# Key tokens by the DMA queue's transposes in place of TensorE's, in a 16-sequence mLSTM and ternary feed-forward block

## The reference, cut to what matters

```
q, k, v = x @ Wq.T, x @ Wk.T, x @ Wv.T           # 256, 256, 512 features
i, f    = soft_cap(x @ Wig.T + big), soft_cap(x @ Wfg.T + bfg)
per token: m' = max(log_sigmoid(f) + m, i);  F = exp(log_sigmoid(f) + m - m');  I = exp(i - m')
           C  = F C + I k v^T;  n = F n + I k
           h  = (q/sqrt(32) . C) / (max(|q/sqrt(32) . n|, exp(-m')) + eps)
x = x + (sigmoid(x @ Wog.T) * head_norm(h) * gamma) @ Wout.T
x = x + gelu(layer_norm(x) @ t(w1).T + b1) @ t(w2).T + b2      # t: absmean ternary
```

## Time and profile before

| what | value |
|---|---|
| time, median of 3 runs | 1792.62 us (1792.32 to 1792.75) |
| profiled execution, its own time | 1793.07 us |
| its span, first to last instruction | 1791.3 us |
| PE busy | 1742.3 us (97%), 12184 matmuls |
| DVE busy | 1412.3 us (79%) |
| ACT busy | 1069.6 us (60%) |
| POOL busy | 604.4 us (34%) |
| mean granted TensorE clock | 0.988 |

### The profile page before, as it was taken

One profiled execution on the slowest core, in us unless ns is written; L12 is line 12 of the kernel. 1 busy time (PEld: TensorE's weight loads), 2 busy tenths in 40 slices (PEclk: granted clock), 3 DMA queues, 4 the chain that ended last, 5 costly groups with the idle time before them and its releaser, 6 DMA issues.

```text
span 1791.3 us, 31686 instructions
## 1 busy us (share of the span) xinstructions
PE 1742.3 (97%) x12184; PEld 868.2 (48%) x12184; DVE 1412.3 (79%) x2526; ACT 1069.6 (60%) x1801; POOL 604.4 (34%) x481
## 2 busy tenths in 40 slices
PE   5879999999999999999999999999999999999999
PEld 3454444444444444444444454444444444444555
DVE  6787878788787878878887887877878787886872
ACT  6877638375573737557373764737466483756743
POOL 1241332524334251432525143252424325242340
PEclk9879999999999999999999999999999999999999
DMA  8433335261432625243262424426243352515120
GB/s 289 167 101 93 85 88 141 54 150 51 122 85 58 163 57 142 62 120 89 54 163 59 128 69 113 106 54 159 54 119 82 97 127 54 133 47 125 32 54 24
DMA packets 255846, 177.76 MB, mean 99 GB/s; under 512 B 200128, under 2 KB 221632, under 8 KB 250576
## 3 DMA queue, kind: packets, MB, share of 16 engines
q1 hardware_dynamic: 254112, 172.59, 37.5%
q10 hardware_dynamic: 1584, 3.15, 0.5%
HBM read 96.47 MB, written 20.23 MB: 65 GB/s over the span
## 4 chain that ended last, share of the span: by engine, by line
PE 74%; ACT 13%; DVE 7%; issue 2%; POOL 1%; DMA 0%; POOLq 0%; DVEq 0%; ACTq 0%
PE pf L2047 23%; PE pf L2031 15%; PE pa L1884 13%; PE pa L1860 9%; PE psh L1884 7%; ACT dec L960 6%; ACT sig L919 2%; DVE gT L1574 2%; PE psh L1987 2%; DVE dec L1460 2%; ACT gT L996 1%; PE pa L1851 1%; ACT L993 1%; ACT g L993 1%; PE psh L2021 1%
## 5 line engine op out<-in xcount | busy, mean ns | idle before, releaser
L2047 PE MATMUL pf<-w2T,gT 128*128 128x512 f16 x2048 | 505.8, 379 | 0.0
L2031 PE MATMUL pf<-x2T,w1T 128*128 128x512 f16 x1920 | 422.0, 379 | 0.0
L2031 PEld LDWEIGHTS pf<-x2T,w1T 128*128 128x128 f16 x1920 | 185.4, 98 | 222.6
L2047 PEld LDWEIGHTS pf<-w2T,gT 128*128 128x128 f16 x2048 | 195.4, 97 | 177.1
L1574 DVE SCALAR_TENSOR_TENSOR gT<-g,wscale,gT 128x512 f16<-128x512 f32 x240 | 203.6, 848 | 68.7 <-ACT gT L996 68.7
L1884 PE MATMUL pa<-wT,xT 128*128 128x512 f16 x960 | 212.9, 379 | 1.0 <-ACT sig L919 0.9
L993 ACT ACTIVATE g<-pf,b1c 128x512 f32<-128x512 f32 x240 | 164.1, 684 | 79.2 <-PE pf L2031 77.1
L1884 PE MATMUL pa<-wT,shared 128*128 128x512 f16 x768 | 178.4, 382 | 1.3 <-DMA shared<-qT 1.3
L996 ACT ACTIVATE gT<-g,wscale 128x512 f16<-128x512 f32 x240 | 173.2, 722 | 7.9
L1001 ACT ACTIVATE ktok<-kT 128x512 f32<-128x512 f32 x64 | 40.3, 630 | 222.3 <-DVE kT L1498 222.3
L1860 PE MATMUL pa<-xT,wT 128*128 128x512 f16 x768 | 172.2, 381 | 0.1
(11 more groups left out here) (242 smaller groups left out, 2774.3 us busy)
## 6 DMA issues: line engine op xcount, KB each, us to landing
dec<-gate_r SPq DMA_DIRECT2D x32, 1024.0 KB, 6.3
xin<-L_attn_x SPq DMA_DIRECT2D x16, 1024.0 KB, 6.1
out<-x1b SPq DMA_DIRECT2D x64, 256.0 KB, 2.2
xres<-L_attn_x SPq DMA_DIRECT2D x16, 512.0 KB, 6.3
xres<-L_attn_x SPq DMA_DIRECT2D x32, 256.0 KB, 3.8
qw<-gate_w SPq DMA_DIRECT2D x128, 48.0 KB, 5.9
s<-state_w SPq DMA_DIRECT2D x60, 97.5 KB, 2.3
qw<-kT SPq DMA_DIRECT2D x120, 48.0 KB, 2.0
```

What stands on the lines that cost most here:

```text
L2031: last = nc.tensor.matmul(bank, w1T[:, k, tok(f)], x2T[:, part, :, k, :], start=(k == 0 and part == HI), stop=(k == KD - 1 and part == LO))
L2047: last = nc.tensor.matmul(bank, gT[:, part, f, tok(t)], w2T[:, f, :], start=(f == 0 and part == HI), stop=(f == NF - 1 and part == LO), sk ...
```

## The change

Key tokens now come from `k_halves` by four DMA transposes that SyncE issues (`key_rows`): one for each part (high, low) and group, [128, 384] f16 each, into `key_parts`, which lies in the memory of `kT`. VectorE adds the two parts and multiplies the sum by the gate factor (`key_tokens`, two instructions over 768 elements). TensorE's six transposes and the two f32 evacuations go. `outer` waits for `ktok_ok`. The keys are no longer scaled back, so the scale of the states' split becomes a constant (STATE_SPLIT), and the factor moves into the scale of the queries (`split_scale[:, 3]`); for b = 0, which has no split queries, `qw` is multiplied by it in place.

SyncE's order: the second norm's transpose comes before the qw loads, and between them the key transposes; for b = 0 the key transposes come behind the qw loads. VectorE's order (b > 0): `key_tokens` behind the norm of the next sequence, `chunk_decay` behind `hidden(0, 1)`, `split_queries` behind `weigh(b, 3)` and not ahead of `weigh(b, 0)`. GpSimd's order (b > 0): the norm's rstd ahead of `weigh_queries`.

```diff
@@ sync, inside gate_rows(b), split in three
+            def key_rows(b):
+                sp.wait_ge(kq_split, at(b, 2, 1))
+                for a in (HI, LO):
+                    for g in range(HG):
+                        sp.dma_start(key_parts[:, a, g, :, :], k_halves[:, a, g, 0:LATE], transpose=True).then_inc(keys_loaded, 16)
+            def query_rows(b):
                 sp.wait_ge(w_stored, at(b, 16, 16))
                 for h in range(H4):
@@ sync, order
             gate_rows(0)
+            query_rows(0)
+            key_rows(0)
...
                 gate_rows(b)
                 transpose_x2(b - 1)
+                key_rows(b)
+                query_rows(b)
                 transpose_x(b + 1)
@@ gpsimd, sequence
                 if first:
                     ternary_low()
+                elif b + 1 < B:
+                    layer_norm(b + 1)
                 weigh_queries(b)
-                if not first and b + 1 < B:
-                    layer_norm(b + 1)
@@ vector
-            def weigh_keys(b, chunks, src, free):
...
+            def key_tokens(b):
+                dve.wait_ge(keys_loaded, at(b, 64, 64))
+                nc.vector.tensor_tensor(ktok[:, :, :].rearrange("p c (g d) -> p g c d", g=HG), key_parts[:, HI, :, :, :],
+                                        key_parts[:, LO, :, :, :], ALU.add).then_inc(keys_sum, 1)
                 dve.wait_ge(ph_free, at(b, PH_USES, U_GT + 1))
...
+                dve.wait_ge(keys_sum, at(b, 1, 1))
+                by_chunk = ktok[:, :, :].rearrange("p c (h d) -> p c h d", d=DQ)
+                nc.vector.tensor_tensor(by_chunk, by_chunk,
+                                        gtok[:, 0:T - 1, ROW_G, :].unsqueeze(3).to_broadcast([P, T - 1, NH, DQ]),
+                                        ALU.mult).then_inc(ktok_ok, 1)
             def chunk_decay(b):
                 dve.wait_ge(w_loaded, at(b, 16 * NH, 16 * NH))
-                nc.vector.tensor_copy(fcol[:, :, :], qw[:, :, P - 1::P]).then_inc(fcol_ok, 1)
+                last = nc.vector.tensor_copy(fcol[:, :, :], qw[:, :, P - 1::P])
+                if isinstance(b, int) and b == 0:
+                    last.then_inc(fcol_first, 1)
+                    dve.wait_ge(fcol_first, 1)
+                    last = nc.vector.tensor_scalar(qw[:, :, :], qw[:, :, :], split_scale[:, 3:4], None, ALU.mult)
+                last.then_inc(fcol_ok, 1)
@@ tensor
             def outer(b):
                 take_ph(b, U_U)
-                pe.wait_ge(ps_free[0], at(b, PS_USES[0], 1))
+                pe.wait_ge(ktok_ok, at(b, 1, 1))
@@ tensor, sequence
-                key_tokens_all(b)
                 for n in range(T):
                     tokens(b, U_O + n, xT[:, :, n, :, :], C_O)
```

More of the change, by code:

```diff
@@ L42 @@
 Q_STACK = 2.0 ** 27
+KEY_SPLIT = 2.0 ** -5
+STATE_SPLIT = 1.0 / (KEY_SPLIT * Q_STACK)
 TINY = 2.0 ** -100
@@ L102, in block_program @@
     PA_USES = U_Y + T
-    PS_USES = (1 + HG, 2 + HG)
-    F_V, F_KEYS, F_SCORES = range(3)
+    PS_USES = (HG, 1 + HG)
+    F_V, F_SCORES = range(2)
     PS_FILLS = F_SCORES + HG
@@ L188, in block_program @@
         cent = [kT[:, i, :] for i in range(2)]
+        key_parts = (kT[:, :, :].bitcast(F16).rearrange("p g s -> p (g s)")[:, 0:2 * HG * LATE]
+                     .rearrange("p (a g t c) -> p a g t c", a=2, g=HG, c=P))
         head_parts = [qT[:, i, :].bitcast(F16).rearrange("p (a d) -> p a d", a=2) for i in range(2)]
@@ L273, in block_program @@
         cst_ok = sem("cst_ok")
+        keys_loaded, keys_sum, ktok_ok = sem("keys_loaded"), sem("keys_sum"), sem("ktok_ok")
+        fcol_first = sem("fcol_first")
         q16_hi, q16_ok, s16_hi, s16_ok = sem("q16_hi"), sem("q16_ok"), sem("s16_hi"), sem("s16_ok")
@@ L596, in _ @@
             transpose_x2(B - 2)
+            key_rows(B - 1)
+            query_rows(B - 1)
             residual(B - 1, RES_TILES[1])
@@ L1196, in scales @@
                     nc.vector.tensor_scalar(evac[:, W_OUT:W_OUT + 1], winv[:, W_OUT:W_OUT + 1], 1.0 / H_SCALE, None, ALU.mult)
-                    nc.vector.tensor_scalar(split_scale[:, 0:1], wscale[:, W_QK:W_QK + 1], 2.0 ** -5, None, ALU.mult)
+                    nc.vector.tensor_scalar(split_scale[:, 0:1], wscale[:, W_QK:W_QK + 1], KEY_SPLIT, None, ALU.mult)
                     nc.vector.tensor_scalar(split_scale[:, 1:2], qk, 2.0 ** -5 / score, None, ALU.mult)
                     nc.vector.tensor_scalar(split_scale[:, 2:3], qk, Q_STACK, None, ALU.mult)
-                    nc.vector.tensor_scalar(split_scale[:, 3:4], wscale[:, W_QK:W_QK + 1], 1.0 / Q_STACK, None, ALU.mult)
+                    nc.vector.tensor_scalar(split_scale[:, 3:4], qk, 1.0 / KEY_SPLIT, None, ALU.mult)
                     nc.vector.tensor_scalar(gcol[:, :], gcol[:, :], wscale[:, W_OUT:W_OUT + 1], None, ALU.mult).then_inc(s_scales, 1)
@@ L1389, in split_parts @@
                                                ALU.mult, ALU.subtract).then_inc(kq_split, 1)
-            def weigh_keys(b, chunks, src, free):
[L1393 to L1399, removed]
-                dve.wait_ge(ph_free, at(b, PH_USES, U_GT + 1))
[L1401 to L1406, removed]
+            def key_tokens(b):
+                dve.wait_ge(keys_loaded, at(b, 64, 64))
+                nc.vector.tensor_tensor(ktok[:, :, :].rearrange("p c (g d) -> p g c d", g=HG), key_parts[:, HI, :, :, :],
+                                        key_parts[:, LO, :, :, :], ALU.add).then_inc(keys_sum, 1)
+                dve.wait_ge(ph_free, at(b, PH_USES, U_GT + 1))
+                dve.wait_ge(keys_sum, at(b, 1, 1))
[3 more added lines that the diff above has]
+                                        ALU.mult).then_inc(ktok_ok, 1)
             def chunk_decay(b):
                 dve.wait_ge(w_loaded, at(b, 16 * NH, 16 * NH))
-                nc.vector.tensor_copy(fcol[:, :, :], qw[:, :, P - 1::P]).then_inc(fcol_ok, 1)
+                last = nc.vector.tensor_copy(fcol[:, :, :], qw[:, :, P - 1::P])
[4 more added lines that the diff above has]
+                last.then_inc(fcol_ok, 1)
             def value_lo(b, t):
@@ L1433, in split_states @@
                 dve.wait_ge(ph_free, at(b, PH_USES, U_U + 1))
-                nc.vector.tensor_scalar(s16[:, HI, :], states, split_scale[:, 3:4], None, ALU.mult).then_inc(s16_hi, 1)
+                nc.vector.tensor_scalar(s16[:, HI, :], states, STATE_SPLIT, None, ALU.mult).then_inc(s16_hi, 1)
                 dve.wait_ge(s16_hi, at(b - 1, 1, 1))
-                nc.vector.scalar_tensor_tensor(s16[:, LO, :], states, split_scale[:, 3:4], s16[:, HI, :],
+                nc.vector.scalar_tensor_tensor(s16[:, LO, :], states, STATE_SPLIT, s16[:, HI, :],
                                                ALU.mult, ALU.subtract).then_inc(s16_ok, 1)
@@ L1599, in sequence @@
                 split_parts(b, ca, U_Q, qT[:, :, :], q_halves, split_scale[:, 1:2])
-                keys_first(b)
-                keys_last(b)
-                chunk_decay(b)
                 if not run_f:
+                    chunk_decay(b)
                     norm_apply(b + 1, range(T))
+                    key_tokens(b)
                     thresholds()
@@ L1614, in sequence @@
                         norm_apply(b + 1, range(T))
+                    key_tokens(b)
+                    if ahead:
                         tokens_split(b + 1)
                     hidden(0, 1)
-                    split_queries(b)
+                    chunk_decay(b)
                 if not run_f:
@@ L1627, in sequence @@
                         hidden(1 + n)
+                    if run_f and n == 3:
+                        split_queries(b)
                     if run_f and n == 4:
@@ L1894, in gate_columns @@
                 last.then_inc(ph_fill, 1)
[L1896 to L1910, removed]
             def outer(b):
                 take_ph(b, U_U)
-                pe.wait_ge(ps_free[0], at(b, PS_USES[0], 1))
+                pe.wait_ge(ktok_ok, at(b, 1, 1))
                 pe.wait_ge(pa_free[pa_bank(b, U_V)], pa_done(b, U_V))
-                pe.wait_ge(ps_free[1], at(b, PS_USES[1], 2))
+                pe.wait_ge(ps_free[1], at(b, PS_USES[1], 1))
                 pe.wait_ge(ph_free, at(b, PH_USES, U_V2 + 2))
@@ L1933, in scores @@
                         take_pa(b, score_use(n))
-                    else:
+                    elif n > 0 or not (isinstance(b, int) and b == 0):
                         pe.wait_ge(ps_free[n % 2], ps_done(b, n) - 1)
```

## The result

The changed kernel takes 1799.14 us (median of 7 runs, 1795.86 to 1800.89) against 1792.75 (7 runs, 1790.61 to 1793.97): ratio 1.0037, interval 1.0026 to 1.0047. It is slower by 6.4 us where 13 us less were forecast. From the gate matmuls of one sequence to those of the next it is 105.4 to 106.9 us, 106.115 in the mean of 14, where before it was 105.68; so each sequence costs 0.44 us more, not 0.90 less.

The account below looks back on a forecast made before the run. TensorE was taken as the bound. 15 steady sequences x 0.90 us = 13.5, less 0.7 for the first, gave -12.8 us: 1779.8 us as median, with a range of 1776.5 to 1784.

Parts of the forecast that it names:

- TensorE is the bound, and the transposes are 0.65 us of it: Steady sequence: PE is busy 105.50 of 105.68 us; dropping its six key transposes gains 0.65 us a sequence.
- The wait of 0.25 us at the second scores goes with the queries' split: Scores of group 1: moving the split behind the fourth `weigh` removes PE's 0.25 us wait; both parts need each other.
- The keys land at 912.4: SyncE's four key transposes: issued by 909.9, landed 2.5 us later at 912.4, between about 911 and 915.6.
- the other end, 4 x 1.30: Key transposes' issue on SyncE: upper end with no saving for the smaller size, keys at 915.6.
- VectorE pays the key instructions from the wait for qw: DVE: about 1.0 us added by the key tokens is paid by the 0.96 us qw wait that leaves.
- From 915.5 on there is a loss, from 916.4 on the change is one: Key arrival: from 915.5 the first loss, from 916.4 the whole change is a loss.
- the slack ahead of `outer` (2.4 us): TensorE's `outer`: `ktok` ready at 915.2, `outer` starting at 917.6, 2.4 us later.
- Rival 3: SyncE's four key transposes run one after another, keys at 917.5: +1.1 us a sequence, 1810 us; chance 0.11.
- The fixed cost of a DMA: Key transposes: a skill's rule of about 2.0 us plus bytes, about 2.2 each, 9 us if paid in turn.
- qw has ample room: SyncE's qw loads: issued from 909.9 to 914.5, landed by about 918, wanted by fcol at 921.3.
- The first sequence, +0.7: First sequence: thresholds stand 1.7 us later behind new DVE work, costing 0.7 us, between 0 and 1.8.
- rival 2: Nothing comes of it: PE's saving is given back at a later wait, about 1793 us; chance 0.09.

Follow-up runs that it names:

- x3: Kernel before with only the new order on VectorE and GpSimd; TensorE's transposes and SyncE's order stay: 1788.91 us, ratio 0.9978.
- x2: Changed kernel with one key transpose of 16 blocks (the last chunk's too) in place of four of 3 blocks: 1778.38 us, ratio 0.9925.
- x11: Changed kernel with two key transposes of 8 blocks (high, low part) in place of four of 3 blocks: 1779.91 us, ratio 0.9935.
- x7: Changed kernel with four key transposes of one block each, VectorE reading the untransposed halves: 1796.45 us, ratio 1.0023.
- x4: Changed kernel, four transposes kept; VectorE splits the next tokens before adding keys, TensorE does `outer` one hidden block later: 1783.53 us, ratio 0.9952.
- x9: Changed kernel with one transpose of 16 blocks and, in the first sequence, thresholds ahead of the key tokens: 1778.14 us, ratio 0.9919.
- x10: x3 plus SyncE's new order (x2T's transpose ahead of the qw loads), key transposes still on TensorE: 1788.89 us, ratio 0.9979.
- x8: Changed kernel with one key transpose of 16 blocks, issued ahead of x2T's transpose: 1780.49 us, ratio 0.9934.

## Why the prediction was wrong

- *TensorE is the bound, and the transposes are 0.65 us of it*: right. Without late keys the period is 104.77, against 104.8 forecast.
- *The wait of 0.25 us at the second scores goes with the queries' split*: right, and independent of the keys: x3, which has the new order of VectorE and GpSimd as a whole, gains it with the transposes still on TensorE. So this part doesn't need the other. Whether the other needs this one, as the prediction says, was not tried.
- *The keys land at 912.4*: wrong, and this is the step that failed. They came at 916.56. The working was 907.9 (x2T's issue over) + 4 x 0.49 + 2.5. Measured were 910.03 + 5.41 + 1.12. Two terms were mis-sized. The larger is the issue of a three-block transpose, scaled down from eight blocks in proportion: 0.49 against 1.26 in the median, 3.4 us in all here. I had the other end, 4 x 1.30, and left it as a bound though it was the nearest row; only the proportion had no row. The smaller is x2T's issue, taken at its old length from a new start: its end came 1.1 us earlier than before, not 3.1. The landing behind the last issue was 1.4 shorter than I took.
- *VectorE pays the key instructions from the wait for qw*: right. The two took 0.96 each, and VectorE was ready for them at 913.2.
- *From 915.5 on there is a loss, from 916.4 on the change is one*: wrong, both some 0.9 too late. I counted the slack ahead of `outer` (2.4 us), but the second scores have less, as x2 and x11 show. In the prediction's count the loss begins at 878.72 + 35.9 = 914.6. The period of before, 105.67, is passed between landings at 36.69 (105.56) and 36.87 (105.73) behind the start, 915.4 to 915.6. With the measured landings and the prediction's own 915.5, 14 sequences would lose 7 us and the kernel would still gain some 5, by an estimate; they lose 18.8 against 104.77. So the late keys are the step that failed, and this mis-sized slack is what turned a smaller gain into a loss.
- *Rival 3* had the outcome (slower) and nearly the arrival (917.5), but the wrong reason: the transposes are not paid one after another in flight. They land 2.4 us after their issue begins while the issues are 1.26 apart, so they overlap.
- *The fixed cost of a DMA* (the Trainium skill, "DMA: Bandwidth & Descriptors", section "Anatomy of one DMA", about 2.0 us plus the bytes): that section is on DMAs that GpSimd issues, and those here are SyncE's. The landing agrees for small ones: 2.3 us for one block (x7) and 2.4 for three (the changed kernel), in the median. For 16 blocks, 512 KB, it would be an estimated 3.2, and 4.4 were measured (x2). That cost is hidden between neighbours. What was not hidden is the time on the queue that issues.
- *qw has ample room*: right while one or no transpose is issued, wrong in x4. The loads land 1.9 us behind their issue in the changed kernel, where before they took 5.9 (medians); the 2.0 in the earlier trace rows is of other DMAs of 48 KB.
- *The first sequence, +0.7*: the thresholds came at 67.3, as forecast (67.4), but TensorE waited 2.8 us for their sum and not 0.9. What that costs in the end stays open (x9).
- *The chances*: the 0.09 for "the same" is rival 2 alone; the weakest cases of rival 3 were named there and counted as slower.

## What to carry to other kernels

An operation that moves to the DMA queue is priced by its issues, one by one, in the order in which that queue's engine makes them, and not by its bytes: take the nearest measured issue as it is, don't scale it down. If it comes out too late, first make fewer and larger ones. A start that is moved forward behind the same backlog ends less early than it starts (2.4 us became 1.7 in x10). And an engine's slack is that of the tightest of all that wait for it further on, not of the first: here the second scores had 0.9 us less than `outer`.

## What the runs showed of the hardware

- A DMA transpose on SyncE takes 1.23 us to issue for one block of 128x128 (median of 64), 1.26 for three, 1.30 to 1.32 for eight, and 2.15 for sixteen (median in x2). The eight-block ones of the earlier trace rows are issued 5 to 8 us apart within a sequence, so the 1.3 us is not a wait for the transpose before.
- The issue of the same 32-block transpose takes 5.6 to 6.6 us with the decays landed and 0.5 MB of loads right ahead of it (x8), and 7.9 to 9.9 right behind 2.5 MB of loads (the changed kernel). SyncE is held meanwhile, with all that stands behind.
- The first sequence has more than one length. TensorE stands idle there for 3.4 to 3.5 us ahead of its first output projection. In the kernel before it then runs at a mean granted clock of 0.61 from 126 to 133 us, and 12 matmuls take 4.96 us; in the profiled execution of the changed kernel the clock is 1.00 and they take 2.75:

```profile
126.00:133.00 7.00, 7.00 (x39) 3.66 (x37) 4.38 (x7) 3.17 (x6) 1.95 (x3) 0.61 0.18 32
```

```profile
126.00:133.00 7.00, 7.00 (x58) 4.17 (x59) 6.82 (x9) 5.14 (x10) 3.19 (x3) 1.00 0.27 57
```

The kernel before has runs near 1790.4 and near 1793, about this far apart. Each kernel has one profile, so that its own runs differ by this is argued from the times and not shown. It would also explain why the changed kernel's profile shows a span only 2.8 us longer, with 14 periods that are 6.1 us longer in sum: its first sequence is 2.3 us shorter (114.10 against 116.42), its last 0.8, and its start comes 0.3 sooner.
